# A graph network kernel on one core: edge attributes in chunks of 64 slots with rings of two, and ScalarE's reading of the sums right behind the scaling

## The reference, cut to what matters

```python
def sage_conv(x, src, dst, W_l, b_l, W_r, n_nodes):
    agg = segment_sum(x[src], dst, n_nodes)
    cnt = segment_sum(ones, dst, n_nodes)
    return (agg / maximum(cnt, 1)) @ W_l.T + b_l + x @ W_r.T
# first network: sage_conv, relu, sage_conv; then x = layernorm(x + result)

def _mp_layer(x, src_f, dst_f, ea_f, W, b):       # ea_f: 16 attributes of each edge, and ones for the loops
    m = concatenate([x[dst_f], x[src_f], ea_f], axis=1) @ W.T + b
    return relu(segment_sum(m, dst_f, n))
# second network: three such layers with batch norms between; then x = layernorm(x + result)
```

## Time and profile before

| what | value |
|---|---|
| median of 3 runs | 1168.71 us (1163.93 to 1168.71) |
| the profiled execution's own time | 1165.03 us |
| its span | 1162.2 us |
| mean granted TensorE clock | 0.928 |
| busy over the span | PE 84%, DVE 63%, ACT 34%, POOL 11% |
| `build` up to the barrier | 0 to 438.2 us |

### The profile page before, as it was taken

How to read it: one execution, slowest core, us unless ns; L and a number is a source line. 1 busy time by engine, 2 the same in 40 slices (tenths; PEclk the granted TensorE clock), 3 DMA queues, 4 the chain that set the end, 5 groups by cost and what they waited for, 6 DMA issues and landing times. The chain is left out here.

```text
span 1162.2 us, 19469 instructions
## 1 busy us (share of the span) xinstructions
PE 972.3 (84%) x7567; PEld 581.9 (50%) x7567; DVE 727.4 (63%) x1415; ACT 395.5 (34%) x808; POOL 128.0 (11%) x150
## 2 busy tenths in 40 slices
PE   0247868878677867999999999998999998999993
PEld 0246767768566754455555444444434443444441
DVE  5797999999999943623433755544464554334434
ACT  1484788787877740200000110113320204210000
POOL 4121313323222220000000000000000000000001
PEclk9768988889888997999999999998999998999996
DMA  6325456555445339983674526665036755037740
GB/s 163 62 71 196 176 169 202 194 180 184 149 143 164 122 126 275 424 281 129 271 318 175 222 89 266 244 246 222 14 124 236 279 207 222 19 144 285 284 164 23
DMA packets 67304, 216.80 MB, mean 187 GB/s; under 512 B 32176, under 2 KB 45227, under 8 KB 53667
## 3 DMA queue, kind: packets, MB, share of 16 engines
q1 hardware_dynamic: 59188, 164.52, 39.7%
q0 software_dynamic: 8016, 50.95, 12.1%
HBM read 170.69 MB, written 44.74 MB: 185 GB/s over the span
## 5 line engine op out<-in xcount | busy, mean ns | idle before, releaser
L1380 PE MATMUL PM<-Aring,Xop 128*128 128x512 fp8e4 (+1 forms) x1960 | 398.7, 363 | 0.0
L1380 PEld LDWEIGHTS PM<-Aring,Xop 128*128 128x128 f16 x1960 | 181.5, 98 | 217.6 <-issue 17.3
L820 PE MATMUL PW<-Aring 128*128 128x52 fp8e4 (+3 forms) x2151 | 121.2, 220 | 79.8 <-ACT F L886 77.7
L820 PEld LDWEIGHTS PW<-Aring 128*128 128x128 fp8e4 x2151 | 114.7, 105 | 84.1 <-ACT F L886 80.4
L1905 ACT ACTIVATE F<-PH,bag 64x512 f32<-64x512 f32 (+1 forms) x39 | 25.5, 658 | 372.0 <-PE PH L1599 371.9
L1380 PE MATMUL PM<-Ares,Xop 128*128 128x512 fp8e4 x588 | 137.1, 388 | 2.8 <-ACT Xop L1944 1.4
L1738 DVE TENSOR_SCALAR S<-PM 128x256 f32<-128x256 f32 (+1 forms) x75 | 31.4, 418 | 112.8 <-PE PM L1380 96.0
L1380 PEld LDWEIGHTS PM<-Ares,Xop 128*128 128x128 f16 x588 | 56.0, 99 | 71.1 <-issue 8.5
L886 ACT ACTIVATE F<-PW 128x392 uint16<-128x392 f32 x196 | 84.5, 511 | 11.4 <-PE PW L820 10.3
L1529 POOL DMA_DIRECT2D out<-dd x12 | 9.1, 757 | 703.7 <-DVE dd L1700 703.7
L678 DVE TENSOR_TENSOR Aring<-Ares 128x4096 uint16<-128x4096 uint16 x31 | 70.8, 2284 | 6.0 <-PE PW L820 5.6
(11 more groups left out here) (158 smaller groups left out, 1204.4 us busy)
## 6 DMA issues: line engine op xcount, KB each, us to landing
Aring<-adj SPq DMA_DIRECT2D x72, 1568.0 KB, 9.8
adj<-Aring POOLq DMA_DIRECT2D x12, 1568.0 KB, 6.4
adj<-Xop POOLq DMA_DIRECT2D x12, 1568.0 KB
Ares<-adj SPq DMA_DIRECT2D x6, 1568.0 KB, 21.5
rc<-ea_sum SPq DMA_DIRECT2D x36, 128.0 KB, 5.5
eaf<-in_erow SPq DMA_DIRECT2D x62, 51.0 KB, 1.9
Aring<-adj SPq DMA_DIRECT2D x4, 784.0 KB, 4.4
rc<-rc_d SPq DMA_DIRECT2D x12, 256.0 KB, 9.5
```

What stands on the lines that cost most here:

```text
L820: last = nc.tensor.matmul(PW[begun % RING][:, c:c + 52 * (z - y)].rearrange("p (d v b) -> p d v b", d=z - y, b=2), lo[:, h % 2, i, :].bitc ...
L1380: last = nc.tensor.matmul(o, x[:, h, :], rhs, start=h == 0, stop=h == NT - 1)
```

## The change

`CH` goes from 32 to 64 slots and `RE` from 4 to 2: 30 chunks instead of 59, one in each of the rounds 1 to 30, and rings of two in `eaf`, `ohd` and `ea_flat`. Each instruction for a chunk is twice as wide. PE raises `s_pp` twice a chunk, behind the first half of its matmuls and at the end, so that `pa_end`, the count for which `sums` waits, is still in steps of about 32 slots; DVE and ACT wait for the whole of chunk c-2. ACT's `sums` moves from the end of an iteration to right behind `low`.

```diff
-CH = 32
+CH = 64
-RE = 4
+RE = 2
 LANDED = [sum(16 * len(PIECES[c]) for c in range(i % RE, i + 1, RE)) for i in range(NCH)]
...
-        ohd = within(2, [128, 4, CH // 2, PD, 2], f16)
+        ohd = within(2, [128, 2, CH // 2, PD, 2], f16)
...
-        ea_flat = sb("ea16", [128, 4, CH // 2 * GW + 62], f16)
+        ea_flat = sb("ea16", [128, 2, CH // 2 * GW + 62], f16)
...
-        pa_end = [max(c for c in range(NCH) for p in PIECES[c] if p[0] // 8 == st) for st in range(NST)]
+        pa_end = [max(2 * c + (2 * i >= len(STEPS[c])) for c in range(NCH) for i, x in enumerate(STEPS[c])
+                      if x[0] // 8 == st) for st in range(NST)]
...
-            return [st for st in range(NST) if pa_end[st] in CHUNKS[h]]
+            return [st for st in range(NST) if pa_end[st] // 2 in CHUNKS[h]]
...
-                if c == NCH - 4:
+                if c == NCH - 2:
                     for i in range(2):
                         sp.wait_ge(s_eo[i], 16 * (EARLY // SW // 2))
...
             def attributes(c):
-                r = c % 4
+                r = c % 2
                 v.wait_ge(s_el[c % RE], LANDED[c])
-                if c >= 4:
-                    v.wait_ge(s_pp, c - 3)
+                if c >= 2:
+                    v.wait_ge(s_pp, 2 * (c - 1))
...
-                    for w, j, e, f, start, stop in STEPS[c]:
+                    for i, (w, j, e, f, start, stop) in enumerate(STEPS[c]):
+                        if i == -(-len(STEPS[c]) // 2):
+                            last.then_inc(s_pp, 1)
...
             def high(c):
-                if c >= 4:
-                    act.wait_ge(s_pp, c - 3)
+                if c >= 2:
+                    act.wait_ge(s_pp, 2 * (c - 1))
...
                 for c in CHUNKS[h] if h < NH else []:
                     low(c)
+                for st in sums_after(h - 1) if h >= 1 else []:
+                    sums(st)
                 if h % 2 == 0 and h // 2 + 1 < TS:
                     across(h // 2 + 1)
...
-                if h >= 1:
-                    for st in sums_after(h - 1):
-                        sums(st)
```

More of the change, by code:

```diff
@@ L832, in _ @@
                             PA[st % 2][:, o:o + 2 * PD].rearrange("p (d e) -> p d e", e=2)[:, :, e:f],
-                            ea_flat[:, c % 4, j * GW:j * GW + 128], ohd[:, c % 4, j, :, e:f], start=start, stop=stop)
+                            ea_flat[:, c % 2, j * GW:j * GW + 128], ohd[:, c % 2, j, :, e:f], start=start, stop=stop)
                     last.then_inc(s_pp, 1)
@@ L875, in low @@
                 act.wait_ge(s_rest, c + 1)
-                nc.scalar.mul(part(c % 4, n, 16), eaf[:, c % RE, 0:n, 0:16].rearrange("p (g s) c -> p g s c", s=2),
+                nc.scalar.mul(part(c % 2, n, 16), eaf[:, c % RE, 0:n, 0:16].rearrange("p (g s) c -> p g s c", s=2),
                               LO).then_inc(s_lo, 1)
```

## The result

The changed kernel takes 1154.44 us (median of 4 runs, 1152.1 to 1155.08), the kernel before 1167.1 us on the same chip (4 runs): a ratio of 0.9888, 95% interval [0.9874, 0.9903], so 13 us faster. On another chip five more runs gave 0.9891 [0.9869, 0.9913]. The forecast was -12.2 us and a median of 1155 us.

The account below looks back on a forecast made before the run. DVE was taken to bound rounds 1 to 30, then a chain through all engines. Terms -9.0 + 1.1 + 0.6 - 2.7 - 0.8 - 1.4 = -12.2 us gave 1152.8, plus 2 for the median: 1155 us; range 1148 to 1163.

Parts of the forecast that it names:

- Widths: DVE's attribute instructions, twice as wide: 0.32 us less in each of 28 rounds, -9.0 us; round 1's extra slots +1.1.
- Rival 2: DVE's attribute instructions: the whole fixed term comes back, no new wait in round 10; -17 us, 1150 us; chance 13%.
- Waits for `high`: L720 on DVE: moved sums let `high` of odd rounds begin earlier, with a new wait in round 10; net -2.7 us.
- Swallowed ahead of other waits: DVE savings just ahead of a wait for PE or ACT are lost, at L678 and one of L702's; +0.6 us.
- The tail: End of `build`: PE waits less for round 29's sums, -0.8 us; POOL adds one stage at its end, not two, -1.4.
- POOL beside DVE and the loads: POOL's stretching of DVE instructions taken as unchanged, 3 us either way in the range; median load landings hidden.
- Sums in odd iterations: ACT's sums now ahead of `first`, `second` and `table`: costed at nothing, +6 us at most.
- rival 3: ACT's queue order: PE's bank stalls reach DVE and odd iterations pay for copies; +17 us, 1184 us; chance 5%.

Follow-up runs that it names:

- the run in halves: Changed kernel with each of DVE's three attribute instructions of a chunk issued in two halves; ratio 1.0002 to the kernel before.
- the tail's second form: Changed kernel with stage 22's sums ahead of `low` in iteration 30, stage 23's behind the first `take` of iteration 31; ratio 0.9835 to the kernel before.
- the tail's first form: Changed kernel with both of iteration 30's sums (stages 22 and 23) ahead of `low` on ACT; ratio 0.9862 to the kernel before.

## Why the prediction was right

The sum was -12.2 us; from round 1 to the barrier the profiles show -11.9, and between the medians lie 12.7. The terms below add up to -11.8, none is off by more than 0.7, and their errors partly cancel. The median of 1155 is closer than the working deserves: the profiled execution was to take 1152.8 us and took 1155.08, 2.3 more, of which 0.9 lie behind the barrier, 0.9 outside the span (3.7 us, not 2.8) and 0.2 ahead of round 1. The 2 us that I put on top for the median made up for that by luck: the median was in fact 0.6 below the profiled execution. Term by term:

- **Widths, forecast -9.0 + 1.1 = -7.9.** Distances of 1.13, 1.14 and 0.29 were forecast and 1.14, 1.14 and 0.29 found. Summed over rounds 1 to 29 (counted as for the run in halves) the attribute instructions went from 83.0 to 74.9 us, -8.1. The run in halves takes this back and with it the gain. Rival 2, in which the whole fixed term of a duration comes back, would have made it -12.3 + 1.1: no.
- **Waits for `high`, forecast -2.7.** They fell from 4.2 to 1.7 us, -2.5, with the new one in round 10 where it was expected: 1.74 for a forecast of 1.3. The reasons held too: the waits of rounds 21, 25 and 29 come back when the even iterations' sums go back, and that of round 11 when stage 1's do.

```profile
162.80 1.05 ACT L873 CAST ea<-eaf 128x1024 f16<-128x1024 f32 x1
163.88 1.23 DVE L721 TENSOR_TENSOR eaf<-eaf,ea 128x1024 f32<-128x1024 f32 x1 [1.74 <-ACT ea L873]
```

- **Swallowed ahead of other waits, forecast +0.6.** It was +1.3: L679's waits went from 5.6 to 6.1, and those of L703 in rounds 1 to 29 from 2.7 to 3.6, most of it in the wait at 146 us, from the first of these rows (before) to the second (after), because DVE arrives earlier at times that PE and ACT set:

```profile
146.22 0.98 DVE L702 TENSOR_SCALAR Aring<-F 128x3136 uint16<-128x3136 uint16 x1 [2.12 <-ACT F L886]
```

```profile
146.33 0.98 DVE L703 TENSOR_SCALAR Aring<-F 128x3136 uint16<-128x3136 uint16 x1 [2.79 <-ACT F L889]
```

- **The tail, forecast -0.8 and -1.4.** PE goes on 3.52 us behind round 30's L713, where it was 4.43 behind the first L712 (-0.9, forecast 3.6), and the rest is 21.81 for 23.13 (-1.3). It is where the forecast had it: from the first `unpack` behind round 30 on, with POOL last and a stage less to add, 1.5 us went; the product behind the stall took 6.98 us for 6.60, which no term had.
- **POOL beside DVE and the loads, forecast at nothing.** Stretched time of DVE in rounds 1 to 29 is 14.2 us and was 14.5; no wait names a load.
- **Sums in odd iterations, forecast at nothing.** No even round but 10 waits for `high`, so the time fits, though no run tests it alone. The reason is incomplete: by the program's order these sums were not free to stay, since with the wide chunks the old place would stop the program (not run), which I had not seen.

What the move is worth was read wrongly. I priced it by `high`, and rival 3, in which a bank's release comes late behind ACT's queue and reaches DVE, got 5 in 100. That is right for the kernel as changed, where the move has removed the mechanism. Undo the move in even iterations, and it is there: 9.5 us in all, more than three times the -2.7 of the term, of which 2.8 are waits for `high` and 5.3 the stall's other two ways to DVE. The parts of the change don't add: the move in all iterations is worth 0.9981 with chunks of 32, and in the even ones alone the step from 0.9964 to 0.9888 with chunks of 64.

## What to carry to other kernels

When a ring is cut from four to two and its unit doubled, look for every wait that stands inside a unit, here PE's wait for a free bank: its releaser may be queued behind something that waits for the end of the same unit, and then the order of that queue decides between a long stall and a short one. Where instructions stand back to back, price their fixed cost by the distance between starts and not by the duration. At the end of a pipeline, take the waits of the last two iterations one at a time; their order was worth 5 to 7 us here, where 28 rounds of wider instructions were worth 9.

## What the runs showed of the hardware

A product of 49 matmuls takes 5.51 us, and after a pause of PE often more. Busy time and granted clock (the third number from the end) of the two products at the end of the changed kernel:

```profile
404.90:411.90 7.00, 7.00 (x53) 5.48 (x50) 0.57 (x2) 1.46 (x4) 0.00 (x0) 0.78 0.02 4
412.40:417.90 5.50, 5.45 (x53) 4.92 (x53) 0.00 (x0) 0.00 (x0) 0.55 (x1) 1.00 0.07 24
```

and, in the run with the tail's second form, of the product of round 27:

```profile
381.20:388.40 7.20, 7.20 (x56) 5.76 (x57) 7.17 (x11) 6.26 (x7) 0.00 (x0) 0.76 0.07 13
```

The lower values are averages over a part at 1.2 and a part at 2.4 GHz. In the changed kernel the granted clock is 0.50 from 402 us, while PE stands still, to 407.5, in the product, and 1.00 from 408.5 us on. In round 27 of the other run it is still 1.00 up to 382 us, behind the end of the stall, and 0.50 from 383 to 385.

Behind the stall of 6.2 us the product took 6.98, 6.98 and 7.03 us in three profiles, behind 5.45 us (before) 6.60, behind 3.9 us (in halves) 7.02, behind 4.8, 6.7 and 7.9 us in two other runs 8.00, 8.10 and 7.00, and behind 1.1 us always 5.51 (five profiles). So a longer stall does not make a longer product. Behind a stall of 3.0 us (in halves, round 27) it took 5.51, and behind the 2.54 us of the tail's first form 7.17. Behind the stall of 2.67 us in round 27 it took 5.51 in six profiles and 7.18 in a seventh, with the same stall and, in three of the six, the same program up to there; what decides there is open. The Trainium skill ("TensorE: Matmul & The Clock Gate", Part 1, on what happens there) says that the monitor behind the clock runs freely and isn't started by the kernel, so that one program can meet it at different moments; the one profile in seven agrees with that, and no run here shows that it is the cause. So a removed stall of PE can give back another 1.5 us through the clock, and two profiles of one kernel can differ by 1.7 us for it.
